# Criss-cross attention on one core: row energies from split keys and queries, in one fp32r pass of 192 columns per row

## The reference, cut to what matters

```python
B, C, H, W = (8, 512, 96, 96);  CQ = C // 8        # 64
q = einsum('oc,bchw->bohw', Wq, x) + bq
k = einsum('oc,bchw->bohw', Wk, x) + bk
v = einsum('oc,bchw->bohw', Wv, x) + bv
energy_H = einsum('bchw,bcgw->bhwg', q, k) - 1e30 * eye(H)   # along a column
energy_W = einsum('bchw,bchv->bhwv', q, k)                   # along a row
att = softmax(concatenate([energy_H, energy_W], -1), -1)
out = gamma * (out_H + out_W) + x      # out_H, out_W: v weighted with the two parts of att
```

## Time and profile before

| | us |
|---|---|
| median of 3 runs | 3722.28 (3722.07 to 3724.83) |
| profiled execution, own time | 3724.42 |
| its span, first to last instruction | 3722.7 |
| PE busy | 3678.4 (99%) |
| DVE busy | 2671.2 (72%) |
| ACT busy | 1535.0 (41%) |
| POOL busy | 631.0 (17%) |

### The profile page before, as it was taken

The page is one execution under the profiler, slowest core; times in us unless marked ns, Lnnn a source line. Parts: engine busy times, 40 slices in busy tenths (PEclk is TensorE's granted clock), DMA queues, the critical chain, the costliest instruction groups (busy, mean ns, idle before and its releaser), DMA issues.

```text
span 3722.7 us, 67097 instructions
## 1 busy us (share of the span) xinstructions
PE 3678.4 (99%) x26968; PEld 3656.7 (98%) x26968; DVE 2671.2 (72%) x4326; ACT 1535.0 (41%) x2134; POOL 631.0 (17%) x792
## 2 busy tenths in 40 slices
PE   8799999999999999999999999999999999999999
PEld 7799999999999999999999999999999999999999
DVE  7767787677876778767786677866778667786555
ACT  8533454244542445424454244542444424444111
POOL 1410023100321003210032100420004200042000
PEclk9899999999999999999999999999999999999999
DMA  8687768877698776977759877697776977769665
GB/s 271 174 229 258 249 214 244 236 251 254 202 250 241 250 244 201 259 234 249 258 184 262 240 252 245 194 267 236 245 256 190 263 228 253 242 206 258 209 210 182
DMA packets 333956, 873.97 MB, mean 235 GB/s; under 512 B 34640, under 2 KB 186704, under 8 KB 333648
## 3 DMA queue, kind: packets, MB, share of 16 engines
q1 hardware_dynamic: 333648, 869.67, 77.0%
HBM read 661.92 MB, written 207.62 MB: 234 GB/s over the span
## 4 chain that ended last, share of the span: by engine, by line
PE 97%; DVE 1%; DMA 1%; ACT 0%; issue 0%; SPq 0%; POOL 0%; DVEq 0%; ACTq 0%; POOLq 0%
PE bank L1029 43%; PE bank L996 18%; PE bank L1017 18%; PE bank L945 10%; PE bank L957 3%; PE bank L966 3%; DMA e_scratch<-E 1%; PE bank L942 0%; DVE E L721 0%; PE bank L981 0%; ACT Sy L591 0%; DVE mx_c L716 0%; DVE Sy L700 0%; DVE zs_c L731 0%; DMA XA<-in_x 0%
## 5 line engine op out<-in xcount | busy, mean ns | idle before, releaser
L1029 PE MATMUL bank<-Sy,Wv_hi 128*128 128x384 f32 x6144 | 1595.7, 340 | 3.8 <-DVE Sy L700 3.6
L1029 PEld LDWEIGHTS bank<-Sy,Wv_hi 128*128 128x128 f32 x6144 | 1086.2, 188 | 8.3 <-issue 4.8
L1029 PE MATMUL bank<-Sy,Wv_lo 128*128 128x384 f32 x3072 | 1028.0, 335 | 0.0
L795 DVE SCALAR_TENSOR_TENSOR Y<-bank,bv_sb,Y 128x384 f32<-128x384 f32 x768 | 470.3, 612 | 718.7 <-PE bank L1029 713.8
L1017 PE MATMUL bank<-Pt,XT 128*128 128x96 f32 x6144 | 715.5, 274 | 0.0
L1017 PEld LDWEIGHTS bank<-Pt,XT 128*128 128x128 f32 x6144 | 713.1, 192 | 0.0
L996 PE MATMUL bank<-Pt,XT 128*128 128x96 f32 x6144 | 691.0, 276 | 2.6 <-DVE Y L779 1.3
L996 PEld LDWEIGHTS bank<-Pt,XT 128*128 128x128 f32 x6144 | 690.0, 193 | 3.2 <-issue 2.2
L462 POOL TENSOR_TENSOR Pe<-Pe,F 128x384 f32<-128x384 f32 x336 | 285.1, 851 | 2385.5 <-DMA Pe<-e_scratch 2354.3
L591 ACT ACTIVATE Sy<-Y 128x768 fp32r<-128x768 f32 x384 | 320.0, 842 | 798.6 <-PE bank L1029 752.3
L1029 PEld LDWEIGHTS bank<-Sy,Wv_lo 128*128 128x128 f32 x3072 | 576.6, 188 | 0.0
(11 more groups left out here) (70 smaller groups left out, 2531.9 us busy)
## 6 DMA issues: line engine op xcount, KB each, us to landing
XT<-in_x_col SPq DMA_DIRECT2D x384, 384.0 KB, 5.9
XT<-in_x_row SPq DMA_DIRECT2D x384, 384.0 KB, 6.0
Y<-in_x SPq DMA_DIRECT2D x192, 768.0 KB, 5.6
out<-Y SPq DMA_DIRECT2D x184, 768.0 KB, 4.3
XA<-in_x SPq DMA_DIRECT2D x180, 768.0 KB, 6.5
e_scratch<-E SPq DMA_DIRECT2D x384, 144.0 KB, 3.1
Pe<-e_scratch SPq DMA_DIRECT2D x336, 144.0 KB, 6.5
XA_first<-in_x SPq DMA_DIRECT2D x12, 768.0 KB, 6.3
```

The source lines that it names most:

```text
L795: nc.vector.scalar_tensor_tensor(at, proj_ps[c % 2][:, 0:CP], bv_sb[:, c:c + 1], at, op0=ALU.add, op1=ALU.add).then_inc(out_made, 1)
L1029: last = nc.tensor.matmul(proj_ps[c % 2][:, 0:CP], w[:, ct, at], Sy[:, lo, ct, :], start=(ct == 0 and k == 0), stop=(ct == CT - 1 and k == 2))
```

## The change

From the second batch on (a >= 1) row energies are made otherwise. `keep_kq` stores keys and queries in full (KQ), `round_kq` reads the same PSUM bank again and writes their fp32r high parts, POOL subtracts to get the low parts (`low_kq`, two instructions), and `copy_k` writes the keys' high part a second time, beside the low queries. q_split holds high queries over low queries, k_split two planes: high keys over high keys, and low keys over zeros. One fp32r matmul per row with 128 partitions and 192 columns gives two halves of 96, whose sum is the energy. The four rows of a chunk go to two banks (`er_halves`, bank 6 and bank 2). DVE adds the halves (two reductions) and takes the maximum (a third). The exponential runs row by row, with the negated maximum as bias and the sum of the row as a second output; so `shift` and `sum_z` go for rows. Bank 2 leaves the rotation of the row products, which has three banks now. The orders of all engines are moved; q_split lies in the memory of Q's second half, so that POOL clears that half once per batch. The prologue's batch 0 keeps the old way.

```diff
-RBANKS = 4
+RBANKS = 3
-        oc_ps, or_ps, proj_ps = (*bank[0:3], bank[5]), (bank[7], *bank[0:3]), bank[3:5]
+        oc_ps, or_ps, proj_ps = (*bank[0:3], bank[5]), (bank[7], *bank[0:2]), bank[3:5]
+        er_halves = (bank[6], bank[2])
...
# SP, row_stage
-                    if a_now and a_now[0]:
-                        store_row_energies(b + 1, a_now[0] - 1)
+                    if more and A_FIRST < n <= A_LAST + 1:
+                        store_row_energies(b + 1, 2 * (n - A_FIRST) - 2)
...
                     if a_now:
-                        store_row_energies(b + 1, a_now[0])
+                        if a_now[0]:
+                            store_row_energies(b + 1, a_now[0] - 1)
...
# POOL
+                if before:
+                    pool.wait_ge(e_summed, past(e_summed, e_no(a, CHUNKS - 1)))
+                    nc.gpsimd.memset(Q[CQ:P, 1, :], 0.0).then_inc(q_zeroed, 1)
+                    pool.wait_ge(q_zeroed, a)
...
+            def low_kq(a, m, last_scaled):
+                pool.wait_ge(p_scaled, past(p_scaled, p_no(a - 1, last_scaled)))
+                if m:
+                    pool.wait_ge(kq_low_made, past(kq_low_made, split_no(a, m - 1) * 2))
+                pool.wait_ge(kq_evicted, past(kq_evicted, a * CHUNKS + m + 1))
+                at = slice(m * CP, (m + 1) * CP)
+                nc.gpsimd.tensor_tensor(q_split[CQ:P, :], KQ[CQ:P, at], k_split[CQ:P, 0, :].bitcast(F32), ALU.subtract)\
+                    .then_inc(kq_low_made, 1)
+                pool.wait_ge(kq_low_made, past(kq_low_made, split_no(a, m) * 2 - 1))
+                nc.gpsimd.tensor_tensor(k_split[0:CQ, 1, :], KQ[0:CQ, at], k_split[0:CQ, 0, :].bitcast(F32), ALU.subtract)\
+                    .then_inc(kq_low_made, 1)
...
                 for n in range(CHUNKS):
+                    if a_now:
+                        low_kq(b + 1, a_now[0], CHUNKS + n + 3)
...
                     if n + 4 < CHUNKS:
                         scale(b, CHUNKS + n + 4)
+                    if a_now:
+                        low_kq(b + 1, a_now[1], CHUNKS + n + 4)
...
# ACT
+            def keep_kq(a, m):
+                act.wait_ge(qk_summed, past(qk_summed, a * CHUNKS + m + 1))
+                if m % 4 == 0:
+                    out_landed(act, a - 1, KQ_SLOT + m // 4)
+                nc.scalar.activation(KQ[:, m * CP:(m + 1) * CP], qk_ps(a, m)[:, 0:CP], ACT.Identity, bias=bqk_sb[:, :])
+
+            def round_kq(a, m):
+                ps = qk_ps(a, m)
+                act.wait_ge(e_summed, past(e_summed, e_no(a, m - 1)))
+                if m == 0:
+                    act.wait_ge(p_turned, past(p_turned, p_no(a - 1, CHUNKS - 1)))
+                nc.scalar.activation(k_split[:, 0, :], ps[:, 0:CP], ACT.Identity, bias=bqk_sb[:, :])
+                nc.scalar.activation(q_split[0:CQ, :], ps[CQ:P, 0:CP], ACT.Identity, bias=bqk_sb[CQ:P, :])\
+                    .then_inc(kq_evicted, 1)
+
+            def copy_k(a, m):
+                act.wait_ge(kq_low_made, past(kq_low_made, split_no(a, m) * 2 - 1))
+                nc.scalar.activation(k_split[CQ:P, 0, :], KQ[0:CQ, m * CP:(m + 1) * CP], ACT.Copy).then_inc(k_copied, 1)
...
+            def row_exponentials(a, m):
+                act.wait_ge(e_maxed, past(e_maxed, e_no(a, m)))
+                for r in range(ROWS):
+                    at, row = slice(m * ROWS + r, m * ROWS + r + 1), by_row(E[0:N, m % ERING, :])[:, r, :, :]
+                    last = nc.scalar.activation(row, row, ACT.Exp, bias=mx_r[:, at], accum_out=zs_r[:, at])
+                last.then_inc(e_exped, 1)
...
                     if a_now:
-                        evict_kq(b + 1, a_now[0])
+                        keep_kq(b + 1, a_now[0])
                         round_x(b + 1, a_now[1])
-                        exponentials(b + 1, a_now[0])
-                        evict_kq(b + 1, a_now[1])
+                        round_kq(b + 1, a_now[0])
+                        if a_now[0]:
+                            row_exponentials(b + 1, a_now[0] - 1)
+                        copy_k(b + 1, a_now[0])
+                        keep_kq(b + 1, a_now[1])
...
                     if a_now and a_now[1] + 1 < CHUNKS:
                         round_x(b + 1, a_now[1] + 1)
+                    if a_now:
+                        round_kq(b + 1, a_now[1])
+                        row_exponentials(b + 1, a_now[0])
...
                     elif n + 1 < CHUNKS:
                         round_y(b, n + 1)
                     if a_now:
-                        exponentials(b + 1, a_now[1])
+                        copy_k(b + 1, a_now[1])
+                    if more and n == A_LAST:
+                        row_exponentials(b + 1, a_now[1])
...
# DVE
+            def add_energies(a, m):
+                dve.wait_ge(e_summed, past(e_summed, e_no(a, m)))
+                if m == 0:
+                    out_landed(dve, a - 1, E_SLOT)
+                e_landed(dve, a, m - ERING)
+                to = by_row(E[0:N, m % ERING, :])
+                for k, ps in enumerate(er_halves):
+                    parts = ps[0:N, 0:2 * HALVES * N].rearrange("p (r h n) -> p r n h", r=2, h=HALVES)
+                    nc.vector.tensor_reduce(to[:, 2 * k:2 * k + 2, :, :], parts, AX_X, ALU.add)\
+                        .then_inc(e_added, 1)
+                dve.wait_ge(e_added, past(e_added, split_no(a, m) * 2))
+                nc.vector.tensor_reduce(mx_r[:, m * ROWS:(m + 1) * ROWS], to, AX_XY, ALU.max, negate=True)\
+                    .then_inc(e_maxed, 1)
...
                         low_x(b + 1, 0)
+                    if a_now and a_now[0]:
+                        add_energies(b + 1, a_now[0] - 1)
                     if a_now:
                         low_x(b + 1, a_now[1])
-                        shift(b + 1, a_now[0])
...
-                    if a_now:
-                        sum_z(b + 1, a_now[0])
...
                     finish(b, n, 2)
                     if a_now:
                         if a_now[1] + 1 < CHUNKS:
                             low_x(b + 1, a_now[1] + 1)
-                        shift(b + 1, a_now[1])
+                        add_energies(b + 1, a_now[0])
...
                         add_row(b, n + 2, 3)
-                    if a_now:
-                        sum_z(b + 1, a_now[1])
+                    if more and n == A_LAST:
+                        add_energies(b + 1, a_now[1])
...
# PE
+            def split_row_energies(a, m):
+                pe.wait_ge(k_copied, past(k_copied, split_no(a, m)))
+                pe.wait_ge(kq_low_made, past(kq_low_made, split_no(a, m) * 2))
+                pe.wait_ge(e_added, past(e_added, split_no(a, m - 1) * 2))
...
+                for r in range(ROWS):
+                    at, to = slice(r * N, (r + 1) * N), slice(r % 2 * HALVES * N, (r % 2 + 1) * HALVES * N)
+                    last = nc.tensor.matmul(er_halves[r // 2][0:N, to].rearrange("p (h n) -> p h n", h=HALVES),
+                                            q_split[:, at], k_split[:, :, at], start=True, stop=True)
                 last.then_inc(e_summed, 1)
...
             def column_energies(a, g):
-                pe.wait_ge(e_shifted, past(e_shifted, e_no(a, CHUNKS + g - 2)))
+                if a and g < 2:
+                    pe.wait_ge(e_exped, past(e_exped, e_no(a, CHUNKS - 1)))
...
                     project(b, n, 0)
-                    if a_now:
-                        row_energies(b + 1, a_now[0])
+                    if a_now and a_now[0]:
+                        split_row_energies(b + 1, a_now[0] - 1)
...
                     project(b, n, 2)
                     if a_now:
-                        row_energies(b + 1, a_now[1])
+                        split_row_energies(b + 1, a_now[0])
...
                         attend_row(b, n + 2, 3)
+                    if more and n == A_LAST:
+                        split_row_energies(b + 1, a_now[1])
```

More of the change, by code:

```diff
@@ L113, in criss_cross_attention @@
         Pt = sb("Pt", [P, 2, CP])
+        with ExitStack() as s5:
+            sb("below_split", [P, CP], F32, s5)
+            q_split = sb("q_split", [P, CP], F32R, s5)
         Q = sb("Q", [P, 2, CP])
+        k_split = sb("k_split", [P, 2, CP], F32R)
         with ExitStack() as s4:
@@ L221, in e_no, with shift_no, split_no @@
             return a * (2 * CHUNKS) + i + 1
+        def shift_no(a, i):
+            return i + 1 if a == 0 else (a + 1) * CHUNKS + i - CHUNKS + 1
+        def split_no(a, m):
+            return (a - 1) * CHUNKS + m + 1
         def p_no(b, i):
@@ L468, in column_stage @@
                     scale(b, g + PRING)
[L470 to L474, removed]
+            def low_kq(a, m, last_scaled):
[9 more added lines that the diff above has]
+                    .then_inc(kq_low_made, 1)
             def row_stage(b, more):
                 scale(b, CHUNKS + 3)
-                if more:
-                    zero_q(b)
                 for n in range(CHUNKS):
```

(40 more changed lines are left out.)

24 lines of the change are left out of this document (12 added, 12 removed).

## The result

| | before | after |
|---|---|---|
| median, us | 3723.11 (4 runs, 3722.07 to 3724.83) | 4107.49 (4 runs, 4097.28 to 4109.54) |
| span of the profiled execution | 3722.7 | 4106.3 |
| mean granted TensorE clock | 0.997 | 0.966 |

The ratio is 1.1026, with a 95% interval of 1.1007 to 1.1046: slower by 10.3%. The forecast was 4170 (3950 to 4330).

What follows compares the result with a forecast made beforehand. PE was taken as the bound, holding 97% of the span. Matmul savings and new waits summed to +53.1 us a batch, +372 in seven, taking 3724.4 to 4096; the clock's +71 gave 4170 us, range 3950 to 4330.

Steps and rivals of the forecast that it cites:

- Part 1: PE's row energies: four fp32r passes of 192 columns replace eight float32 passes, 0.37 us a chunk for 0.71, 0.34 saved.
- Part 2: DVE: add_energies takes 1.61 us in place of shift (1.13) and sum_z (0.48); each adding reduction taken at 0.55.
- Part 3: ACT: one more PSUM read, copy_k, and four exponentials with row sums at 0.50 us each, 2.0 a chunk.
- Part 4: POOL: two subtractions a chunk, 0.83 us each; overlapping low_x, they cost DVE 0.4 and 0.3 us.
- The waits: PE pauses: project_kq for low_x 1.32 us; fourth row product for add_row 3.77, last iteration 1.75; column energies for gather_q 3.5.
- The clock: TensorE's granted clock after the 84 new pauses of some 3.5 us: half of them cost 1.7 us, +71 us.
- rival (b): The clock falls at nearly every pause, 84 x 1.7 to 3.4 us: 4240 to 4380 us, chance 0.22.
- rival (a): The forecast itself, PE's new waits plus clock loss at half the pauses: own range 4080 to 4240 us, chance 0.48.
- a period near 22 us: Sign to look for: A iterations go from 17.48 to 21.9 us, with an unchanged period elsewhere.
- Costing nothing: Three banks in other iterations, SP's moved stores and queued x loads, the prologue's extra copy, the scratch: no cost.
- (d): Faster: PE stays the bound, the two pauses of an iteration adding up to under 0.68 us; 3667 us, chance 0.07.
- (c): Small operations are cheap, POOL takes no share and the clock holds: 3881 us, up to 4080, chance 0.20.

Runs made afterwards that it cites:

- mended kernel: The kernel after, operations, banks and buffers kept, with other orders on DVE, ACT, SP and PE (3694.6 us), then two more moves on ACT and DVE: 3673.0 us, ratio 0.9867.

## Why the prediction was right

The direction, the three places, their counts and the size were right; two terms were off, one up and one down. Against the steps of the prediction:

- **Part 1.** 0.34 us saved per chunk forecast; 0.35 measured. The mended kernel's whole gain, 50 us, agrees with the 57 forecast less remainders of a few microseconds.
- **Part 2.** Each adding reduction took 545 ns for 0.55 taken, although it has 192 outputs and a long stride. `add_energies` took 1.52 us to the next start (1369.91 to 1371.43) for 1.61. The 0.48 taken for a reduction was misread: the rows from 1304.50 to 1304.98 show the subtraction of `shift`. It did no harm, since two adding reductions start 0.47 apart (two of 0.545 in 1.01 us).
- **Part 3.** 2.0 us for four exponentials was too much: they take 1.45. The row sum is an instruction of its own, as I took it to be, but it hides in its neighbours. The groups after (busy us, mean ns, idle before):

```profile
L616 ACT ACTIVATE E<-E,mx_r 96x96 f32<-96x96 f32 x672 | 243.3, 363 | 263.8 <-DVE mx_r L798 263.8
L616 ACT ACTIVATION_READ_ACCUMULATOR E<-E,mx_r 96x1 f32 x672 | 125.3, 186 | 0.0
L795 DVE TENSOR_REDUCE E<-bank 96x192 f32<-96x384 f32 x336 | 169.7, 545 | 0.0
L493 POOL TENSOR_TENSOR q_split<-KQ,k_split 64x384 fp32r<-64x384 f32 x168 | 366.0, 2178 | 1266.9 <-ACT q_split L596 1266.9
L757 DVE TENSOR_TENSOR Sx<-XA,Sx 128x768 fp32r<-128x768 f32 x342 | 316.4, 965 | 1.7 <-ACT Sx L572 1.7
```

  A pair is issued every 0.36 us. The Trainium skill's price (ScalarE: Activation LUTs, What ACT_TABLE_LOAD costs), an estimated 1.16 us for four without the sum, was nearer than mine.
- **Part 4.** The step that failed in kind. The two engines do get in each other's way, but here it is POOL that stands: the first subtraction of a chunk takes 2.18 us on average (3.05 at the first place, 1.51 at the second), while the second, beside no `low_x`, takes 1.0 and `low_x` keeps its 0.97. The 0.83 charged for a subtraction was too low even for one left alone. The 0.4 and 0.3 us charged to DVE were nothing in the steady iterations. Only in the first A iteration of each batch do two halves of `low_x` take 2.63 instead of 1.82 us. The Trainium skill's rule (SBUF: State Buffer, Who interferes with whom) names the pair rightly. It adds that the order of issue decides who blocks, a half that I had left out; by the starts that this trace records it does not show. POOL's subtraction starts first in both cases, 0.35 us ahead of `low_x` (1361.73 and 1362.08) where POOL stands, and 0.23 us ahead of its second half (1339.88 and 1340.11) where DVE does. Starts and ends on POOL are rough in this profile, and no run separates the two cases.
- **The waits.** For low_x 1.32 forecast, 0.89 measured (1363.17 less 1360.19 and a block of 2.08); for the third bank 3.77 and 2.76, of which 0.55 are the exponentials, 0.3 POOL, the rest `add_energies` and hand-overs; in the last A iteration 1.75 and 1.0; at the column energies 3.5 and 2.6. Per batch that is -8.2 + 11 x 0.89 + 11 x 2.76 + 1.0 + 2.6 = +35.6, in seven batches +249 where +372 was forecast. The row products' starts show somewhat more, -0.63 + 11 x 3.17 + 4.32 = +38.6 a batch and +270 in seven: each of the two project_kq blocks of a full iteration takes 0.1 us longer than its 2.08.
- **The clock.** Half of the pauses at 1.7 us, +71, was too little. The price was about right (22.28 less 20.65 is 1.63; 1.5 on average over all 77), but the clock fell in most A iterations: 113 us, and 3 at the column energies of two batches. That was rival (b)'s mechanism, on shorter pauses than it was priced for. 270 + 116 = 386 for the 384 us measured. So the forecast of 4170 came out 62 too high from two errors, 102 us too much for the waits and 45 too little for the clock, that partly cancelled; the rest is the 1.3 us between the two starting times and rounding. That the time also fell into the narrower range of rival (a) is in part luck. So is the sign "a period near 22 us": the forecast had 21.9 from waits alone, and the measured 22.12 is 20.65 from waits and 1.47 from the clock.
- **Costing nothing.** Three banks elsewhere, SP's order, the prologue and the scratch: none shows among PE's waits. Three banks alone cost the iterations outside the A iterations nothing, as forecast (0.6 us in all between the row products' starts); the experiment on them expected 13 us at most in the A iterations, and they cost 21.

The rivals: (d), faster, needed both pauses to add up to less than 0.68 us, and they are 3.65; it is what the mended orders gave. (c) had the right size for part of its terms and the wrong sign for the clock.

## What to carry to other kernels

When a rotation of buffers loses one, follow the release of the buffer backwards through every engine's order, not only its own: here `add_row` stood behind reductions on DVE and exponentials on ACT that nobody was waiting for, and they cost the row products nothing while there was a fourth bank. Work that is moved should be placed behind whatever feeds the bounding engine soonest, on each engine that it visits. And a pause of PE can have two prices, its own length and the clock that follows: here the pauses of 2.8 us had both, those of 0.9 us only the first. Take either away and look at the clock before judging the other, since the clock can eat a gain whole.

## What the runs showed of the hardware that was not expected

- **The clock and the length of a pause.** In otherwise dense A iterations, pauses of 0.7 us shown never brought the clock down (with the exponentials behind round_y: two in each of 77 iterations), and pauses of 2.6 us shown did in 65 of 77 iterations (after). With 2.8 us shown it was 76 of 77, and the loss by the mean clock rose from 140 to 201 us (with `low_x` first).
- **Idle matmuls pay.** 20 matmuls into unused columns, 2.2 us per iteration, made the kernel 101 us faster (mean clock 0.994 instead of 0.966).
- **POOL held by DVE.** A subtraction on POOL that takes 1.0 us elsewhere stretched to 3.05 us where two halves of `low_x` ran. In the first A iteration of a batch it is the second half of `low_x` that stretches, to 1.77 us (timelines of POOL and DVE after; first the first A iteration, then the one behind it):

```profile
1339.25 2.63 DVE L757 TENSOR_TENSOR Sx<-XA,Sx 128x768 fp32r<-128x768 f32 x2
1339.88 1.18 POOL L493 TENSOR_TENSOR q_split<-KQ,k_split 64x384 fp32r<-64x384 f32 x1 [15.49 <-ACT q_split L596]
...
1361.73 3.05 POOL L493 TENSOR_TENSOR q_split<-KQ,k_split 64x384 fp32r<-64x384 f32 x1 [12.09 <-ACT q_split L596]
1362.08 1.81 DVE L757 TENSOR_TENSOR Sx<-XA,Sx 128x768 fp32r<-128x768 f32 x2
1364.86 1.01 POOL L496 TENSOR_TENSOR k_split<-KQ,k_split 64x384 fp32r<-64x384 f32 x1
```

- **Short fp32r passes.** 192 columns with 96-column weights take 0.09 us each, half of what 384 columns take; no penalty for the width shows.
